# A transformer layer on one core: projection and FFN blocks issued in one piece per step, one phase of a block per step

## What is computed

```
x: (16, 1024, 256) fp32, 16 heads of 16
q, k, v = x Wq' + bq, x Wk' + bk, x Wv' + bv     # RoPE on q and k, q times 16**-0.5
o = softmax(q k') v, per head, over all 1024 positions
h = layernorm(x + o Wo' + bo)                    # no gain, no offset
f = relu(h T(W1)' + b1)                          # 1024 wide, T: ternary weights
out = layernorm(h + f T(W2)' + b2)
```

## Time and profile before

| what | us |
|---|---|
| median of three runs | 3700.4 |
| lowest and highest run | 3691.02, 3704.95 |
| time of the profiled execution | 3703.57 |
| span of the profiled execution | 3701.8 |
| PE busy | 3512.3 |
| DVE busy | 3021.1 |
| ACT busy | 2744.8 |
| POOL busy | 1929.2 |

### The profile page before, as it was taken

The page is one execution under the profiler, slowest core; times in us unless marked ns, Lnnn a source line. Parts: engine busy times, 40 slices in busy tenths (PEclk is TensorE's granted clock), DMA queues, the critical chain, the costliest instruction groups (busy, mean ns, idle before and its releaser), DMA issues.

```text
span 3701.8 us, 79641 instructions
## 1 busy us (share of the span) xinstructions
PE 3512.3 (95%) x30726; PEld 1830.9 (49%) x30726; DVE 3021.1 (82%) x5619; ACT 2744.8 (74%) x5320; POOL 1929.2 (52%) x1831
## 2 busy tenths in 40 slices
PE   4888999999999999999999999999999999999985
PEld 3433455555555555555555555555555555544444
DVE  4867888888888888888888888888888888888711
ACT  2267788878877887788778878887888788777751
POOL 2143456556655655565556555655565566533326
PEclk7689999999999999999999999999999999999977
DMA  5233433443444344434443443344344434442210
GB/s 149 48 83 73 109 87 89 104 112 84 91 105 105 87 95 106 98 95 93 107 94 98 90 110 91 93 96 112 88 88 105 112 85 91 102 92 56 54 39 24
DMA packets 292284, 336.89 MB, mean 91 GB/s; under 512 B 59712, under 2 KB 241856, under 8 KB 291648
## 3 DMA queue, kind: packets, MB, share of 16 engines
q1 hardware_dynamic: 291904, 331.79, 39.1%
HBM read 193.27 MB, written 138.41 MB: 90 GB/s over the span
## 4 chain that ended last, share of the span: by engine, by line
PE 87%; ACT 5%; POOL 3%; DVE 2%; issue 2%; DMA 1%; SPq 0%; POOLq 0%; DVEq 0%; ACTq 0%
PE sc L604 35%; PE ob L621 27%; PE job L499 22%; ACT prob L711 5%; PE ms L593 2%; DVE mxp L974 1%; POOL hid_r L1036 1%; DVE mxp L827 0%; POOL ka L1102 0%; DMA xt_sb<-xt 0%; DMA qa<-qk_parts 0%; POOL hid_r L1034 0%; PE sc L499 0%; POOL xt_r L1017 0%; POOL parts L331 0%
## 5 line engine op out<-in xcount | busy, mean ns | idle before, releaser
L711 ACT ACTIVATE prob<-sc 128x512 f32<-128x512 f32 x4096 | 2363.7, 600 | 789.5 <-PE sc L604 698.9
L827 DVE TENSOR_REDUCE mxp<-ms 128x1 f32<-128x512 f32 x4032 | 2581.2, 684 | 433.2 <-PE ms L593 410.6
L604 PE MATMUL sc<-qa,ka 50*128 50x512 f32 x4096 | 1856.4, 464 | 78.9 <-ACT prob L711 41.3
L593 PE MATMUL ms<-ka,qa 48*128 48x512 f32 x4032 | 1823.9, 465 | 2.6 <-DVE mxp L827 1.7
L604 PEld LDWEIGHTS sc<-qa,ka 50*128 50x128 f32 x4096 | 753.4, 186 | 1355.9 <-ACT prob L711 985.3
L621 PE MATMUL ob<-prob,v_sb 128*17 128x512 f32 x8192 | 1090.7, 605 | 2.3 <-ACT at_st L717 2.3
L593 PEld LDWEIGHTS ms<-ka,qa 48*128 48x128 f32 x4032 | 741.0, 185 | 14.7 <-DVE mxp L827 13.4
L1028 POOL TENSOR_TENSOR rstd<-ve,half_sb 128x2 f32<-128x2 f32 x128 | 88.9, 694 | 835.9 <-DVE ve L864 835.9
L1036 POOL TENSOR_TENSOR hid_r<-hid,hid_r 128x512 fp32r<-128x512 f32 x256 | 328.9, 1285 | 20.5
L499 PE MATMUL job<-h_t,w_sb 64*128 64x256 f32 x3840 | 317.4, 281 | 0.0
L499 PE MATMUL job<-w_sb,hid_r 64*128 64x256 f32 x3840 | 312.0, 278 | 0.0
(11 more groups left out here) (93 smaller groups left out, 2562.3 us busy)
## 6 DMA issues: line engine op xcount, KB each, us to landing
qk_parts<-parts SPq DMA_DIRECT2D x128, 512.0 KB, 4.5
ka<-qk_parts SPq DMA_DIRECT2D x384, 128.0 KB, 4.6
qa<-qk_parts SPq DMA_DIRECT2D x384, 128.0 KB, 7.5
attention<-at_st SPq DMA_DIRECT2D x128, 256.0 KB, 3.0
v_ones<-v_st SPq DMA_DIRECT2D x64, 272.0 KB, 3.3
v_sb<-v_ones SPq DMA_DIRECT2D x64, 272.0 KB, 8.6
xt_sb<-xt SPq DMA_DIRECT2D x64, 256.0 KB, 6.9
xn<-x SPq DMA_DIRECT2D x64, 256.0 KB, 6.4
```

What stands on the lines that cost most here:

```text
L593: nc.tensor.matmul(ms[upto(b, g, NS1, at) % MS_BANKS][:, :], operand(qa, b, g, j, ROWS)[:, qt * P:(qt + 1) * P], operand(ka, b, g, j, ROWS ...
L604: nc.tensor.matmul(sc[upto(b, g, HG * STEPS, n) % SC_BANKS][:, :], operand(ka, b, g, j, ROWS + MROWS)[:, tt * P:(tt + 1) * P], operand(qa, ...
L711: nc.scalar.activation(prob[st_ % 2][:, j, :], sc[upto(b, g, HG * STEPS, n) % SC_BANKS][:, :], ACT.Exp).then_inc(s["exp_done"], 1)
L827: nc.vector.reduce_max(mxp[:, kh, j * TT + qt:j * TT + qt + 1], ms[upto(b, g, NS1, at) % MS_BANKS][:, :], AX.X).then_inc(s["s1_taken"], 1)
```

## The change

- A step's job stands at one place, behind the second score pair, and is one phase of a whole block: `e0` is phase 0 of all of e and `e1` its phase 1 (12 matmuls each), likewise `o0`, `o1`, and `v`, which now takes two steps, `v0` and `v1`. `g0` and `g1` are phase 0 of the first and second half of the hidden units, `g2` and `g3` phase 1 (16 matmuls each; new function `second_layer`).
- `t3` is one step in place of two. It and `f0` to `f3` keep both phases in one step, behind the second and the fourth pair (`IN_TWO_PLACES`). t4 stands behind the second pair.
- The tables shift: e and o one step earlier, v from step 11 to steps 6 and 7, t4 from 6 to 5, f from 7-10 to 8-11; g stays in 12-15. The second projection of units 0 and 1 starts in step 8. `SPLIT_STEP` goes from 13 to 14, `SECOND_SPLIT_STEP` from 6 to 5.
- ACT empties jobs behind its fourth exponential (t4: behind the second), and `take_outputs` stands ahead of the first exponential. DVE's sums of t3 and the first norm's steps come earlier.
- In the units with two projections SP issues the next unit's token load (`proj_in`) ahead of `attention_in` and of the last `proj_out`, which waits for POOL; before it stood behind them.
- In the last part the four g pieces of a quarter are made by one call at `g3`, behind a wait for all hidden units.

```diff
-PROJ_JOBS = {1: [{2: "e0", 3: "e1", 4: "o0", 5: "o1", 11: "v"}],
-             2: [{2: "e", 3: "o", 4: "v"}, {9: "e", 10: "o", 11: "v"}]}
-TAIL_JOBS = {0: "t3a", 1: "t3b", 6: "t4", 7: "f0", 8: "f1", 9: "f2", 10: "f3", 12: "g0", 13: "g1", 14: "g2", 15: "g3"}
-SPLIT_STEP = 13
-SECOND_SPLIT_STEP = 6
+PROJ_JOBS = {1: [{1: "e0", 2: "e1", 3: "o0", 4: "o1", 6: "v0", 7: "v1"}],
+             2: [{0: "e0", 1: "e1", 2: "o0", 3: "o1", 4: "v0", 5: "v1"}, {8: "e0", 9: "e1", 10: "o0", 11: "o1", 12: "v0", 13: "v1"}]}
+TAIL_JOBS = {0: "t3", 5: "t4", 8: "f0", 9: "f1", 10: "f2", 11: "f3", 12: "g0", 13: "g1", 14: "g2", 15: "g3"}
+IN_TWO_PLACES = ("t3", "f0", "f1", "f2", "f3")
+SPLIT_STEP = 14
+SECOND_SPLIT_STEP = 5
...
-FIRST_NORM = {(2, 1): "stats 0", (2, 3): "stats 1", (3, 1): "moments 0"}
+FIRST_NORM = {(0, 3): "sums", (1, 1): "stats 0", (1, 3): "stats 1", (2, 1): "moments 0"}
...
                 store_attention(b, g, 0)
+                for at in projected_next(b, g)[:1 if len(proj) > 1 else 0]:
+                    proj_in(*at)
                 if prepared(b, g)[0] >= 0:
                     attention_in(*prepared(b, g))
                 for at in proj[-1:]:
                     proj_out(*at)
-                for at in projected_next(b, g)[:1 if len(proj) > 1 else 0]:
-                    proj_in(*at)
...
+            def second_layer(b, g, phase, hidden, bank_free, end=False):
+
+                banks = [bank[:, 0:TQ] for bank in banks_of("g", end)]
+                for what, n in bank_free:
+                    wait_used(pe, s[what], n)
+                if phase == 0:
+                    pe.wait_ge(s["hid_low"], upto(b, g, FT // 2, hidden[-1] // 2 + 1))
+                terms = [[(hid_r[part][:, f, tl * P:(tl + 1) * P], w2_sb[:, f, :]) for tl in range(TL)]
+                         for f in hidden for part in range(2)]
+                last = in_halves(banks, terms, phase, hidden[0] == 0, hidden[-1] == FT - 1)
+                if phase == 1 and hidden[-1] == FT - 1:
+                    last.then_inc(s["t6_ready"], 1)
+                    return [("t6_taken", upto(b, g, TL, TL))]
+                return []
...
-            def run(job_, phase, free):
+            def run(job_, place, free):
+
                 stage, at, name = job_
-                return {"proj": proj_job, "tail": tail_job}[stage](*at, name, phase, free)
+                if stage == "proj":
+                    return proj_job(*at, name[0], int(name[1]), free) if place == 1 else free
+                if name[0] == "g":
+                    part = int(name[1])
+                    return second_layer(*at, part // 2, range(part % 2 * FT // 2, (part % 2 + 1) * FT // 2), free) if place == 1 else free
+                if name in IN_TWO_PLACES:
+                    return tail_job(*at, name, place // 2, free) if place in (1, 3) else free
+                return tail_job(*at, name, 0, free) if place == 1 else free
...
-                        scores(b, g, st_, 0, tiles[0])
-                        if job_:
-                            free = run(job_, 0, free)
-                        scores(b, g, st_, 1, tiles[1])
-                        if not job_:
-                            weigh_before(b, g, st_, first)
-                        scores(b, g, st_, 2, tiles[2])
-                        if job_:
-                            free = run(job_, 1, free)
-                        scores(b, g, st_, 3, tiles[3])
-                        if job_:
-                            weigh_before(b, g, st_, first)
+                        for j in range(HG):
+                            scores(b, g, st_, j, tiles[j])
+                            if job_:
+                                free = run(job_, j, free)
+                            if j == (3 if job_ else 1):
+                                weigh_before(b, g, st_, first)
...
-                        exps(b, g, st_, 0)
                         if st_ == TT + 1:
                             take_outputs(b, g, 0)
                         if st_ == 1 and not (first and g == 0):
                             take_outputs(b + (g - 1) // G, (g - 1) % G, 1)
+                        job_ = job_at(b, g, st_, tail)
+                        exps(b, g, st_, 0)
                         exps(b, g, st_, 1)
+                        if job_ and job_[2] == "t4":
+                            finish(job_)
                         exps(b, g, st_, 2)
-                        job_ = job_at(b, g, st_, tail)
-                        if job_:
-                            stage, at, name = job_
-                            {"proj": proj_job, "tail": tail_job}[stage](*at, name)
                         exps(b, g, st_, 3)
+                        if job_ and job_[2] != "t4":
+                            finish(job_)
```

More of the change, by code:

```diff
@@ L488, in _, with in_halves @@
             halves = [0]
-            def in_halves(banks, terms, phase, first=True, last=True, turn=0):
-                if phase == 1:
+            def in_halves(banks, terms, phase, first=True, last=True):
+                if phase == 1 and first:
                     pe.wait_ge(s["halves_done"], halves[0])
@@ L501, in in_halves @@
                                                 stop=(last and phase == 1 and n == len(terms) - 1))
-                if phase == 0:
+                if phase == 0 and last:
                     halves[0] += 1
@@ L505, in in_halves, with proj_job @@
                 return done
-            def proj_job(b, g, name, phase, bank_free):
-                kind, begins, ends = name[0], name[1:] != "1", name[1:] != "0"
-                if phase == 0 and begins:
+            def proj_job(b, g, kind, phase, bank_free):
+                if phase == 0:
                     if kind == "e":
@@ L522, in proj_job @@
                             terms.append([(wqk_r[wp][:, c, i, "eo".index(kind), :], xt_r[xp][:, c, :]) for i in range(2)])
-                if not (begins and ends):
-                    terms = terms[0:3] if begins else terms[3:6]
-                last = in_halves([bank[:, 0:TQ] for bank in job], terms, phase, begins, ends, int(not begins))
+                last = in_halves([bank[:, 0:TQ] for bank in job], terms, phase)
                 full = {"e": "even", "o": "odd", "v": "v"}[kind]
-                if phase == 0 or not ends:
+                if phase == 0:
                     return bank_free
@@ L534, in tail_job @@
                 if phase == 0:
[L535 removed]
+                    if name == "t3":
                         pe.wait_ge(s["att_done"], upto(b, g, 1, 1))
@@ L555, in tail_job @@
                     return [("t4_taken", upto(b, g, 2, 2))]
[L556 to L560, removed]
+                if name == "t3":
+                    terms = [[(att_t[:, c, tl * P:(tl + 1) * P], wo_sb[:, c, :]) for tl in range(TL)] for c in range(KC)]
+                    last = in_halves(banks, terms, phase)
                     ready, free = "t3_ready", [("t3_taken", upto(b, g, TL, TL))]
-                elif name[0] == "f":
+                else:
+                    n = int(name[1])
                     terms = [[(w1_sb[:, c, f * P:(f + 1) * P], h1_t[part][:, c * TQ:(c + 1) * TQ]) for f in (2 * n, 2 * n + 1)]
@@ L567, in tail_job @@
                     ready, free = "f_ready", [("f_taken", upto(b, g, FT // 2, n + 1))]
[L568 to L575, removed]
+                if phase == 0:
+                    return bank_free
                 last.then_inc(s[ready], 1)
                 return free
+            def second_layer(b, g, phase, hidden, bank_free, end=False):
+                banks = [bank[:, 0:TQ] for bank in banks_of("g", end)]
+                for what, n in bank_free:
+                    wait_used(pe, s[what], n)
+                if phase == 0:
+                    pe.wait_ge(s["hid_low"], upto(b, g, FT // 2, hidden[-1] // 2 + 1))
[6 more added lines that the diff above has]
+                return []
             def whole(job_, *args):
@@ L699, in _, with finish @@
                     bank = banks_of(name, True)[0].name
-                    frees[bank] = whole(tail_job, B - 1, g, name, frees.get(bank, []), True)
+                    if name[0] == "g":
+                        if name == "g3":
+                            for phase in range(2):
+                                frees[bank] = second_layer(B - 1, g, phase, range(FT), frees.get(bank, []) if phase == 0 else [], True)
+                    elif name == "t4":
+                        frees[bank] = tail_job(B - 1, g, name, 0, frees.get(bank, []), True)
+                    else:
+                        frees[bank] = whole(tail_job, B - 1, g, name, frees.get(bank, []), True)
         @block.scalar
         def _(act):
+            def finish(job_):
+                stage, at, name = job_
+                {"proj": proj_job, "tail": tail_job}[stage](*at, name)
             def exps(b, g, st_, j):
@@ L795, in _ @@
             for g in range(G):
-                for name in ("e", "o", "v"):
```

(5 more changed lines are left out.)

15 lines of the change are left out of this document (4 added, 11 removed).

## The result

The changed kernel took 3640.0 us, median of four runs (3629.8 to 3648.61). The kernel before, run beside it, took 3695.71, median of four (3689.74 to 3704.95). The ratio is 0.9846, 95% interval 0.9808 to 0.9884: faster by 1.5%. The forecast was 3645.

The account below looks back on a forecast made before the run. PE's order of work sets the pace. From 3703.6 us: -49 for units 4 to 57, -22 first batch row, +2 units 58 to 63, +13 last part, giving 3648, or 3645 as median of runs; range 3620 to 3684.

Parts of the forecast that it names:

- Steps by prices: Steady units: step times built from prices read off the timeline, 53.3 us before and 52.1 after, ahead of handovers.
- The floor of 1.18 and 1.67: Each step: third and fourth scores cannot start sooner, held by two `sc` banks and ACT's exponentials; job steps at least 3.09.
- The 0.3 for handovers: Steady units: us added per unit for e0 needing t3's sums and tiles bunching on three `ms` banks; bounds 0 and 0.6.
- The cover of `att_t`: Before t3: POOL's `att_t` still ready ahead of use, some 1.2 us left, 1.0 if ACT's copy comes later.
- The first batch row: Units 0 to 3: token-load waits go (-12), steps behind recover up to 9, less +5 and -6; together -22 us.
- The +5 for a falling clock in units 2 and 3: Units 2 and 3: nine steps in a row without a job may lower PE's clock, costing 5 us.
- the -6 for the order of the steps: First batch row: copies of `ob` and the double units' long steps give 1.5 us per unit, -6.
- The last part: Kernel's end: all g matmuls start behind POOL's last low part; +13 us, from +3 to +18.
- The case with the low clock: Last part: PE's clock falls while idle, g takes about 7.3 us, t4 4.3 late three times, 16 us before t3's 2.5.
- DVE's (two): Steady units: DVE becomes the bound, 0.6 us more per unit, 3677 us; chance 0.10.
- The same-half boundary's (three): Scores behind a job ending in their array half start late, 0.2 a boundary, about 1.1 per unit, 3704 us; chance 0.07.
- Rival four: Before t3: `att_t` comes late from POOL and stops PE once per unit; at 2.6 us late, 3741 us; chance 0.06.

Follow-up runs that it names:

- Experiment 3: Changed kernel with the second phase of f0 to f3 behind the third score pair instead of the fourth: 3598.63 us, ratio 0.9714 to the kernel before.
- experiment 4: Changed kernel with each score exponential over only 256 of its 512 columns, half the probabilities left out: 3456.92 us, one run.
- experiment 5: Changed kernel with g as before, eight matmuls behind the first and eight behind the third score pair: 3696.74 us, ratio 0.9985 to the kernel before.
- experiment 8: Changed kernel with f's second phase behind the third pair and last part's g in four pieces: 3580.78 us; then step 9's `ob` copy behind the second exponential: 3574.13.
- experiment 6: Changed kernel with `SPLIT_STEP` at 15 instead of 14, so POOL's split_x and normalise come one step later: 3882.51 us, one run.
- experiment 1: Kernel before with only the token load moved ahead of attention_in and the last proj_out on SP: 3685.8 us, ratio 0.9946 to the kernel before.
- Experiments 2: Changed kernel with the last part's g in four pieces again, each behind its own hidden units: 3624.73 us, ratio 0.9783 to the kernel before.
- experiment 7: Changed kernel with 72 unread matmuls added on PE ahead of each g call of the last part: 3636.5 us, ratio 0.9821 to the kernel before.

## Why the prediction was right

The time, 3640 for 3645, and the sign came out of four terms that each came near: -45.4 for -49, -24.7 for -22, +0.2 for +2 (all of units 58 to 63), +12.4 for +13. Not all of them came near for the reason given.

- *Steps by prices.* The floor of 1.18 and 1.67, 0.118 for two matmuls and 0.99 for `weigh` gave 3.09 for o, v and g and 3.56 for f; the medians are 3.08 to 3.09 and 3.55 to 3.56. Experiment 3 changed the order once more and gave 3.30 for f; experiment 4 took the floor away. Of all that the change does to steady units, g is what pays: experiment 5, +55 without it. By the medians of steps, e and o gain 0.3 (for 0.5) and t3 2.9 (for 3.0), v's second step takes 2.6, and t4 and f together 0.6.
- *The 0.3 for handovers* was the right size with other contents. t3 took 3.95 for 3.87: its second phase stands behind a pair that had waited for ACT, and that takes 0.34, not 0.24. e0 took 3.18. Step 9 took 3.65: I had costed ACT's copy ahead of the first exponential at nothing, since ACT waits for PE there, but it delays the exponentials by which the third scores are released (1.28 in this step, 1.18 in the other f steps). In the changed kernel that costs 0.09 a unit; with f placed as in experiment 3 it costs 0.29, which experiment 8 takes back. The kernel before paid 0.27 for its copy in step 9 (3.58, where the f steps beside it took 3.31), and the forecast had read its five t4 and f steps only as a sum.
- *The cover of `att_t`* was 0.57 for 1.0. POOL's wait for ACT shrank from 3.59 to 2.65 as one expects of one step less before a longer step 0; the rest of the miss I have not taken apart. It cost nothing, and experiment 6 shows how close it was: one step less, and it costs five times the unit's gain of 0.84.
- *The first batch row.* The end of the waits was right, 12.1 for 12 in step 14 of units 0 and 1; the steps behind gave 6.6 for up to 9, and units 0 to 3 in all 16.8. The +5 for a falling clock in units 2 and 3 was wrong: it stayed full from 196 us on, though nine steps in a row had no job. With that the -6 for the order of the steps was too small in units 1 to 3, which are 14.8 shorter than in experiment 1. In the first profile after, a slow unit 0 hid this: the sum of -24.7 is nearer to -22 than its parts are.
- *The last part.* The case with the low clock came true: t4 6.2 behind POOL, where I had 2.9 + 4.3 = 7.2 with the low clock all through (it came back within the call) and 4.1 without. 3.3, 3.2 and 3.1 in the first three quarters, 4.7 in the last and t3's -2.5 give 11.8, and 12.4 were measured. Experiments 2 and 7 take it apart: 15.2 us for the call in one piece, at least 5.1 of it by the clock, since in the last quarter experiment 7 did not keep the clock up.
- *Rivals.* DVE's (two) would have shown idle time of PE ahead of maximum tiles; the page has 2.3 us in all. The same-half boundary's (three) would have put third scores later than 0.34 + 0.24 + 0.94 in g steps; the row shows 1.51, to 0.01. The Trainium skill (TensorE: Matmul & The Clock Gate, Part 3, "The mechanism") has the rule that a weight load overlaps only with matmuls in another row group. The traces speak against it as the forecast read it: no price is visible at these boundaries, and the weights of g0's third scores load from 1821.46 to 1821.65, under two job matmuls, one in each half, that run from 1821.46 to 1821.74. Rival four stood 0.57 us of cover away, and its price left the clock out: experiment 6 shows 2.0 us a unit beside the wait.

## What to carry to other kernels

Where a ring of two banks between two engines sets a floor in each step, filler work is free only in front of the tile that the floor holds back: put it there, and look for what the floor still leaves before you split it (f: 3.56, 3.30 with the second group moved by one pair). A copy costed at nothing because its engine waits must be held against what that engine releases next, not against its idle time. And where a change merges pieces, look for the same code at the ends of the kernel, where pieces followed their producer: merging gave 0.9 us a unit and took 15 at the end.

## What the runs showed of the hardware

- Nine steps in a row without filler did not lower the clock in the changed kernel (units 2 and 3 at 1.00), though it fell in the same units of experiment 1, and in unit 3 of experiment 4 (from 325.3 us for 10.2). One wait of 2.34 us in a unit that is otherwise fully busy lowered it in 50 of 54 units of experiment 6 (0.57 in a stretch of 4 us behind one), and added 2.0 us to the 2.5 that the wait costs by itself (4.5 a unit in all).
- A job's matmuls in twos take 0.118 us a pair at the full clock and 0.21 to 0.22 at half, read from the g call of the last part, whose rows at 3547.76 and 3547.97 are one such distance.
- A score pair that had to wait costs its successor 0.1 us: 0.34 in place of 0.24 (t3's second phase, 1781.72 to 1782.06 in the changed kernel, against 0.24 in g0), and `weigh` 0.43 in place of 0.33.
